# Feed-forward and output projection two chunks behind the attention; the right-hand matrix quantised beside chunks 0 to 2

## The chip, the cores and the metric

One Trainium2 chip runs the program on eight cores at once. A core has five engines with a program each: PE (TensorE, matmuls and transposes), DVE (VectorE), ACT (ScalarE), POOL (GpSimd) and SP (SyncE, which here only issues DMAs). They meet through semaphores. The metric is the device time of the slowest core in microseconds.

## The reference

```
x  [16, 2048, 1024]
xn = layernorm(x)
q, k, v = xn @ Wq.T, xn @ Wk.T, xn @ Wv.T      # 16 heads of 64
a  = softmax(q k / 8, position i sees i-127 .. i) v
s  = a @ Wo.T
ql = clip(round(xn / lhs_scale)), lhs_scale = max|xn| over the row / 127
qr = clip(round(rhs / rhs_scale)), rhs_scale = max|rhs| over the column / 127
g  = silu((ql @ qr) * lhs_scale * rhs_scale)
out = x + s * g
```

Each core has two of the 16 sequences, that is 4096 rows, and all five weight matrices of 1024 x 1024.

## The kernel before

The rows are worked on in 32 chunks of 128 (`NC`); two chunks make a span. A chunk c needs: the layer norm (`bn` the statistics, `rstd` the root on POOL, `xn` the normalised tile in bf16), its transpose (`TX`), Q and K for a span (`Q`, `K`, four groups each), V (`V`, two halves), the attention in four steps b of four heads (`S` scores, `exp` on ACT, `msk` on DVE, `A` product with V, `norm` on DVE), the quantised left-hand tile (`cen` on ACT, `amax` on DVE, `qp` on ACT, `ql` on DVE) and its transpose (`TL`), the feed-forward product (`F`, two halves: `zev` on DVE, `th` on ACT, `gate` on DVE), the output projection (`O`, two halves: `t1` on DVE, `add` on POOL) and the store. `t_xn`, `t_ql` and `t_ao` are DMA transposes that SP issues from chunk 4 or 6 on; before that PE transposes.

All orders are written out by hand. `pe_order` gives PE's list: a start in which Q, K, V follow the arrival of the weights, then for each chunk four slots. A slot is scores (c, b), the attention product of the step before, and the groups that `slot_gaps(c)` names for it. Before, F is of the same chunk and O of the one before; in a middle chunk the four slots hold two of Q or K; two of Q or K and V half 0; V half 1 and F half 0; F half 1 and both O.

Groups go to PSUM banks in turn: four banks `pj` for the ordinary ones, and in the start four more (`pav`, `psc`, list `early`). `before[g]` is the group four places back in the same list, and `pe_ready` lets g start only when that one has been emptied. Who empties is in `evacuator`: DVE for F and O, ACT for V, Q and K of later spans. `emit_vector`, `emit_scalar` and `emit_gpsimd` walk through the same slots; what a slot's groups leave for DVE comes after `msk`, `bn` or `xn` and `amax` of that slot, and the last one of a chunk is held until the next slot begins.

The right-hand matrix (`rhst`) comes in eight blocks. `rabs` and `rscale` (DVE) find the scales, `rq` (ACT) and `rcast` (POOL) quantise, `TR` transposes on PE, `RS` with `rdiag` spreads the scales. The staging tiles `stage` borrow `gg`, `zz`, `tt` and `xr`; the rounded blocks borrow `aot` and `ao`. `load_w` issues weight blocks from POOL; they are converted to bf16 on the way.

## Time and profile before

| what | value |
|---|---|
| times of three runs | 710.5, 711.29, 712.15 us; median 711.29 |
| the profiled execution | 712.11 us, span of the slowest core 710.5 us |
| spans of the eight cores | 703.9 to 710.5 us |
| granted TensorE clock, by core | 0.985 to 0.989 |
| PE busy | 665.4 us, 94% |
| DVE, ACT, POOL busy | 475.9, 346.7, 172.6 us |
| DMA moved | 86.40 MB |

The span is the time from the first to the last instruction of a core. The granted clock is 1.00 at 2.4 GHz, 0.5 at 1.2 GHz; a mean between is a mixture. A timeline row gives the start in us from the span's beginning, the length, the engine, the line and operation, output and inputs with their tile names, and how many equal instructions were merged; what stands in brackets is how long the engine was idle before it, and what ended that.

### The profile page before, as it was taken

The numbers are of one execution on the slowest core, as the hardware profiler recorded it, in microseconds if no ns is written. First come the engines' busy times: TensorE is split into PE (matmuls) and PEld (weight loads), VectorE is DVE, ScalarE is ACT, GpSimd is POOL, SyncE is SP. The second block draws the span as 40 slices with busy tenths as digits, with TensorE's granted clock in tenths as the row PEclk, the third lists the DMA queues.
The fourth block names the chain that finished last, engine by engine and source line by source line (L and its number), as shares of the span: only waits on it lengthen the run. The fifth ranks groups of instructions, "written<-read, shape, count | busy, mean of one in ns | idle before, by whom it ended". The sixth has DMA issues, their size and how long they took to land.

```text
span 710.5 us, 17009 instructions; the slowest of 8 cores (703.9 to 710.5 us)
## 1 busy us (share of the span) xinstructions
PE 665.4 (94%) x5724; PEld 413.0 (58%) x5724; DVE 475.9 (67%) x958; ACT 346.7 (49%) x473; POOL 172.6 (24%) x281
## 2 busy tenths in 40 slices
PE   1897769989999999999999999999999999999995
PEld 0682436555666666565666666565666666556642
DVE  4644577766776677766766667766766677664485
ACT  1342665544554445554554445554554445453442
POOL 4323311322222222121222222121222222120122
PEclk9998979999999999999999999999999999999999
DMA  9999913735655454656757445545555445543234
GB/s 191 149 200 188 182 18 76 149 119 134 134 129 127 119 88 97 131 120 134 134 120 127 115 102 94 130 120 134 135 122 125 115 92 104 131 89 76 76 90 149
DMA packets 109859, 86.40 MB, mean 122 GB/s; under 512 B 92112, under 2 KB 92240, under 8 KB 109776
## 3 DMA queue, kind: packets, MB, share of 16 engines
q1 hardware_dynamic: 104880, 76.83, 47.4%
q0 software_dynamic: 4608, 8.39, 8.4%
q8 instruction: 49, 0.80, 0.5%
q14 instruction: 34, 0.28, 0.1%
q10 hardware_dynamic: 288, 0.10, 0.1%
HBM read 54.62 MB, written 16.78 MB: 100 GB/s over the span
## 4 chain that ended last, share of the span: by engine, by line
PE 87%; DVE 5%; DMA 4%; issue 2%; POOL 1%; ACT 1%; DVEq 0%; SPq 0%; ACTq 0%; POOLq 0%
PE pj L675 44%; PE pj L666 29%; PE psc L759 5%; PE pav L783 4%; PE pav L785 2%; DMA xs<-x 2%; DMA wv<-wvt 2%; DVE ee L356 1%; PE pav L666 1%; PE psc L666 1%; DVE sm L326 1%; DVE gg L385 0%; DVE sm L291 0%; DVE sm L403 0%; POOL aot L831 0%
## 5 line engine op out<-in xcount | busy, mean ns | idle before, releaser
L573 ACT ACTIVATE ee<-psc 128x1024 bf16<-128x1024 f32 (+1 forms) x128 | 128.4, 1003 | 157.8 <-PE psc L759 152.9
L825 POOL TENSOR_TENSOR xr<-tt,xr 128x512 f32<-128x512 f32 x63 | 80.4, 1277 | 370.0 <-DVE tt L391 344.6
L675 PE MATMUL pj<-wv,xnt 128*128 128x512 bf16 x480 | 118.7, 391 | 5.1 <-DMA wv<-wvt 3.8
L675 PE MATMUL pj<-qrhs,qlt 128*128 128x512 bf16 x512 | 122.0, 382 | 0.0
L675 PE MATMUL pj<-wo,aot 128*128 128x512 bf16 x512 | 116.4, 379 | 1.2 <-ACT aot L313 1.2
L666 PE MATMUL pj<-xnt,wq 128*128 128x256 bf16 x960 | 112.3, 276 | 1.9 <-DVE xnt L311 1.8
L666 PE MATMUL pj<-xnt,wk 128*128 128x256 bf16 x960 | 109.7, 273 | 0.0
L356 DVE TENSOR_TENSOR ee<-ee,mask_s 128x1024 bf16<-128x1024 bf16 (+1 forms) x128 | 104.1, 813 | 7.6 <-ACT ee L573 2.1
L666 PEld LDWEIGHTS pj<-xnt,wq 128*128 128x128 bf16 x960 | 93.1, 99 | 13.5 <-issue 2.1
L666 PEld LDWEIGHTS pj<-xnt,wk 128*128 128x128 bf16 x960 | 92.0, 98 | 10.3
L675 PEld LDWEIGHTS pj<-wo,aot 128*128 128x128 bf16 x512 | 49.5, 98 | 60.0 <-issue 1.7
L391 DVE TENSOR_TENSOR tt<-pj,gg 128x512 f32<-128x512 f32 x64 | 44.0, 690 | 54.4 <-PE pj L675 53.4
L675 PEld LDWEIGHTS pj<-qrhs,qlt 128*128 128x128 bf16 x512 | 48.3, 99 | 54.3 <-issue 2.8
L675 PEld LDWEIGHTS pj<-wv,xnt 128*128 128x128 bf16 x480 | 45.9, 100 | 53.1 <-issue 12.0
L539 ACT ACTIVATE xs<-xs,sm 128x1024 f32<-128x1024 f32 x32 | 36.6, 1148 | 75.5 <-DVE xnr L321 75.5
L367 DVE TENSOR_TENSOR ao<-pav,sm 128x256 bf16<-128x256 f32 x128 | 54.4, 425 | 13.3
L326 DVE TENSOR_REDUCE sm<-xs 128x1 f32<-128x1024 f32 x32 | 39.0, 1218 | 34.9 <-ACT xs L539 34.9
L759 PEld LDWEIGHTS psc<-qt,kt 64*128 64x128 bf16 x992 | 28.1, 94 | 49.6 <-issue 49.4
L378 DVE SCALAR_TENSOR_TENSOR zz<-pj,sm,rsb 128x512 f32<-128x512 f32 x64 | 47.8, 747 | 10.7 <-PE pj L675 7.8
L759 PE MATMUL psc<-qt,kt 64*128 64x128 bf16 x992 | 50.1, 219 | 2.5 <-ACT ee L573 2.5
L783 PE MATMUL pav<-vv,ee 128*128 128x65 bf16 x480 | 46.5, 196 | 6.0 <-DVE ee L356 3.4
L556 ACT CAST kt<-pj 128x512 bf16<-128x512 f32 x60 | 33.6, 582 | 32.2 <-PE pj L666 32.2
(122 smaller groups left out, 661.5 us busy)
## 6 DMA issues: line engine op xcount, KB each, us to landing
xs<-x SPq DMA_DIRECT2D x32, 512.0 KB, 6.7
xr<-x SPq DMA_DIRECT2D x32, 512.0 KB, 7.2
y<-xr SPq DMA_DIRECT2D x31, 512.0 KB, 8.2
wq<-wqt POOLq DMA_DIRECT2D x8, 256.0 KB, 10.4
wk<-wkt POOLq DMA_DIRECT2D x8, 256.0 KB, 11.1
wv<-wvt POOLq DMA_DIRECT2D x8, 256.0 KB, 8.3
wo<-wot POOLq DMA_DIRECT2D x8, 256.0 KB, 10.1
xr<-rhst SPq DMA_DIRECT2D x3, 512.0 KB, 5.8
```

The costliest lines, as they stand in the source:

```text
L326: op(lambda: v.reduce_max(col(c, AMAX), xs[c % XS][:], AX.X, apply_absolute_value=True), "v")
L356: op(lambda: v.tensor_tensor(a, a, m, ALU.mult), "v", ("mask", c, b))
L367: op(lambda: v.tensor_tensor(view(ao[c % 2], b * 256, (64, 4), (1, 64)), view(p, 0, (66, 4), (1, 64)), bass.AP(sm, C_RS + 4 * (b % 2), [[1 ...
L378: op(lambda: v.scalar_tensor_tensor(zz[h], banks[bank["F", c, h]], col(c, LSH), rsb[:, h * 512:(h + 1) * 512], ALU.mult, ALU.mult), "v", ( ...
L391: op(lambda: v.tensor_tensor(tt[h], banks[bank["O", c, h]], gg[c % 2][:, h * 512:(h + 1) * 512], ALU.mult), "v", ("ev", "O", c, h))
L539: op(lambda: a.activation(xs[c % XS][:], xs[c % XS][:], AF.Identity, scale=-1.0, bias=col(c, MEAN)), "a", ("cen", c))
L573: op(lambda: a.activation(o, i, AF.Exp, scale=0.125), "a", ("exp", c, b))
L666: yield [(lambda kc=kc, m=m: t.matmul(p[:, m * 256:(m + 1) * 256], w[:, kc * 1024 + (2 * j + m) * 128:kc * 1024 + (2 * j + m + 1) * 128], ...
L675: yield [lambda kc=kc: t.matmul(p[:], src[:, off + kc * step:off + kc * step + 128], w[:, kc * 1024 + j * 512:kc * 1024 + (j + 1) * 512], ...
L759: todo.append(lambda m=m, kk=kk, ko=ko, rows=rows, q0=q0: t.matmul(psc[:, q0:q0 + 128], kk[rows, m * 256 + ko:m * 256 + ko + 128], qt[s % ...
L783: todo.append(lambda out=out, e0=e0, vp=vp: t.matmul(out, e[:, e0:e0 + 128], vp, start=True, stop=False))
L825: op(lambda: p.tensor_tensor(r, tt[h], r, ALU.add), "p", ("add", c, h))
```

## The change

- F and O are worked on in the slots of the chunk two later (`LAG`), through the whole program. Chunks 30 and 31 hold F and O of 28 and 29; F and O of 30 and 31 follow the last attention product (`last_groups`), and the last chunk's attention output is transposed by DMA like the others (`TA` goes).
- A middle chunk's four slots hold: F half 0 and one of Q or K; F half 1 and two of Q or K; the fourth of Q or K, V half 0 and O half 0; V half 1 and O half 1.
- x of chunks 0 to 3 is loaded in halves of 64 partitions, one half issued by SP and one by ACT. POOL issues the first Wq blocks once the first half of x(0) has landed, and Wk and Wv without a wait for `rhst`.
- The V groups of chunks 0 to 3, which came before the attention, now lie in the slots of chunk 0. `rhst` is loaded after Wv; its blocks are quantised in chunks 1 and 2, now with `rq_p` and `rcast` both on POOL, into other borrowed tiles. Wo is issued last, in two fours between those operations.
- Transposes of xn and ql for chunks 4 and 5 are emptied by ACT; those of ql go up to chunk 5 (`NTL`). Rings for small values and for ql transposes get longer (`NSM`, `QLR`). Statistics of chunk c + 4 begin in chunk 3.

```diff
@@ -16,12 +16,12 @@
...
-XS, XR, QLR, VR, NSM = 4, 3, 6, 6, 6
+XS, XR, QLR, VR, NSM, LAG = 4, 3, 7, 6, 8, 2
...
-C_MAGIC, C_NHALF, C_RST, C_RAM, C_RSC, C_RS = 144, 146, 148, 156, 164, 176
-NPRE, NTL = 6, 4
+C_MAGIC, C_NHALF, C_RST, C_RAM, C_RSC, C_RS, SMT = 192, 194, 196, 204, 212, 224, 240
...
@@ -47,22 +47,29 @@
...
     x = [("KQ"[c % 2 == 0], s + 1, g) for g in range(4)]
-    v, f, o = halves("V", c + 2), halves("F", c), halves("O", c - 1)
+    v, f, o = halves("V", c + 2), halves("F", c - LAG), halves("O", c - LAG)
     if c == 0:
-        return [halves("TX", 4, 5), halves("V", 4)[:1], halves("V", 4)[1:], []]
+        v2, v3 = halves("V", 2), halves("V", 3)
+        return [v2 + halves("TX", 4), v3 + halves("TX", 5), halves("TL", 4, 5), []]
     if c == 1:
-        v, f1 = halves("V", 5), [("F", i, 1) for i in range(2)]
-        return [halves("TR", 4, 5), v[:1] + halves("TR", 6, 7), v[1:] + [("RS", 0, 1)] + f1[:1], f1[1:]]
+        v4, v5 = halves("V", 4), halves("V", 5)
+        return [v4[:1], v4[1:] + halves("TR", 0, 1), v5[:1], v5[1:] + halves("TR", 2, 3)]
     if c == 2:
-        o0 = halves("O", 0)
-        return [x[:2], x[2:] + o0[:1], o0[1:] + o[:1], o[1:] + f]
+        return [x[:1] + [("RS", 0, 0)] + halves("TR", 4), x[1:2] + halves("TR", 5), x[2:3] + halves("TR", 6),
+                x[3:] + halves("TR", 7) + [("RS", 0, 1)]]
     if c == 3:
-        return [x[:2], x[2:], f[:1], f[1:] + o]
-    if c == NC - 2:
+        f0, o0 = halves("F", 0), halves("O", 0)
+        return [f0[:1] + x[:1], f0[1:] + x[1:2], f[:1] + x[2:3], x[3:] + f[1:] + o0]
+    if c == 4:
+        return [halves("O", 1) + x[:1], f[:1] + x[1:3], f[1:] + x[3:] + v[:1], v[1:] + o]
+    if c >= NC - 2:
         return [f[:1], f[1:], o[:1], o[1:]]
-    if c == NC - 1:
-        return [f[:1], f[1:], o[:1] + [("TA", c, 0)], o[1:] + [("TA", c, 1)]]
-    return [x[:2], x[2:] + v[:1], v[1:] + f[:1], f[1:] + o]
+    return [f[:1] + x[:1], f[1:] + x[1:3], x[3:] + v[:1] + o[:1], v[1:] + o[1:]]
+def last_groups():
+    return [g for k in "FO" for g in halves(k, *range(NC - LAG, NC))]
...
@@ -71,33 +78,27 @@
...
-    v0, v1 = halves("V", 0, 1), halves("V", 2, 3)
+    v0 = halves("V", 0, 1)
     each = lambda gs, steps: [("G", [g], steps) for g in gs]
-    out = one(halves("TX", 0, 1)) + [("G", q0, range(4))] + one(halves("TX", 2)) + [("G", q0, range(4, 5))]
-    out += one(halves("TX", 3)) + [("G", q1, range(5)), ("G", q0, range(5, 6)), ("G", q1, range(5, 6))]
-    out += each(q0 + q1, range(6, 8))
+    out = one(halves("TX", 0, 1)) + [("G", q0, range(6))] + one(halves("TX", 2, 3))
+    out += each(q0, range(6, 8)) + each(q1, range(8)) + one(halves("TL", 0, 1))
     out += [("G", k0, range(4)), ("G", k1, range(4))] + each(k0 + k1, range(4, 8))
-    out += one(halves("TL", 0, 1))
-    out += [("G", v0, range(4)), ("G", v1, range(4))] + each(v0 + v1, range(4, 8))
-    out += one(halves("TL", 2, 3) + halves("TR", 0, 1, 2, 3) + [("RS", 0, 0), ("F", 0, 0), ("F", 1, 0)])
-    for c in range(NC):
+    out += one(halves("TL", 2, 3))
+    first = slot_gaps(0)
+    for b, ks in enumerate((range(3), range(3, 6), range(6, 8))):
+        out += [("S", 0, b), ("G", v0, ks)]
+    out += [("A", 0, 0)] + one(first[0]) + [("S", 0, 3), ("A", 0, 1)] + one(first[1]) + [("A", 0, 2)] + one(first[2])
+    for c in range(1, NC):
         for b, gap in enumerate(slot_gaps(c)):
-            out.append(("S", c, b))
-            if b:
-                out.append(("A", c, b - 1))
-            elif c:
-                out.append(("A", c - 1, 3))
-            out += one(gap)
-    last = halves("O", NC - 1)
-    out += [("A", NC - 1, 3)] + one([("TA", NC - 1, 2)])
-    out += [("G", [g], range(6)) for g in last] + one([("TA", NC - 1, 3)])
-    out += [("G", [g], range(6, 8)) for g in last]
-    return out
+            out += [("S", c, b), ("A", c, b - 1) if b else ("A", c - 1, 3)] + one(gap)
+    return out + [("A", NC - 1, 3)] + one(last_groups())
...
+    if k in ("TX", "TL") and i >= 4:
+        return "a"
...
@@ -117,8 +118,8 @@
...
-    early = halves("TX", 2, 3) + [("Q", 1, g) for g in range(4)] + [("K", 1, g) for g in range(4)]
-    early += halves("V", 2, 3) + halves("TL", 2, 3) + halves("TR", 0, 1, 2, 3) + [("RS", 0, 0)]
+    wide = halves("TX", 2, 3) + halves("TL", 0, 1, 2, 3) + [(k, 1, g) for k in "QK" for g in range(4)]
+    early = [g for g in groups if g in wide]
@@ -195,23 +196,28 @@
...
+        def load_half(eng, c, h):
+            r = slice(h * 64, h * 64 + 64)
+            op(lambda: eng.dma_start(xs[c][r, :], x_h[c * 128 + h * 64:c * 128 + h * 64 + 64, :]),
+               f"{('lx', 'lh')[h]}{c}", c, 16)
...
@@ -248,37 +254,48 @@
         def load_rh(sync, i):
             if i == 7:
-                need(sync, "p", ("rcast", 3))
-            op(lambda: sync.dma_start(stage[i][:], rhst_h[i * 128:(i + 1) * 128, :]), f"rh{i % 7}", i, 16)
+                need(sync, "p", ("rcast", 0))
+            op(lambda: sync.dma_start(stage[i], rhst_h[i * 128:(i + 1) * 128, :]), f"rh{i}", 0, 16)
...
             for c in range(4):
-                load_x(sync, c)
-            landed(sync, "wk4", 0)
+                load_half(sync, c, 0)
+            landed(sync, "wk5", 0)
+            load_x(sync, 4)
+            load_x(sync, 5)
+            landed(sync, "wv4", 0)
             for i in range(4):
                 load_rh(sync, i)
-            landed(sync, "wv2", 0)
-            load_x(sync, 4)
-            load_x(sync, 5)
-            landed(sync, "wv6", 0)
+            load_x(sync, 6)
             for i in range(4, 8):
                 load_rh(sync, i)
-            load_x(sync, 6)
-            for c in range(NC):
...
-                    t_ao(sync, c - 1)
-                if 2 <= c < NC - 5:
+            load_x(sync, 7)
...
@@ -442,60 +458,61 @@
...
             evac_v(v, ("TL", 1, 0))
-            rabs(v, 3)
-            rscale(v, 2)
-            rdiag(v, 0)
             bn(v, 4)
             bn(v, 5)
+            evac_v(v, ("K", 1, 0))
+            evac_v(v, ("K", 1, 1))
+            xn(v, 4)
+            evac_v(v, ("K", 1, 2))
+            evac_v(v, ("K", 1, 3))
             evac_v(v, ("TL", 2, 0))
             evac_v(v, ("TL", 3, 0))
-            for i in range(4):
-                evac_v(v, ("TR", i, 0))
-            xn(v, 4)
             xn(v, 5)
-            rabs(v, 4)
-            zev(v, 0, 0)
-            rabs(v, 5)
-            rscale(v, 4)
-            gate(v, 0, 0)
-            zev(v, 1, 0)
-            rabs(v, 6)
-            gate(v, 1, 0)
-            extra = {(0, 1): [(rabs, 7), (rscale, 6)], (0, 2): [(rdiag, 1)], (0, 3): [(amax, 4)], (1, 1): [(ql, 4)],
-                     (1, 2): [(amax, 5)], (2, 0): [(ql, 5)]}
+            amax(v, 4)
+            msk(v, 0, 0)
+            amax(v, 5)
+            msk(v, 0, 1)
+            ql(v, 4)
+            msk(v, 0, 2)
+            ql(v, 5)
+            norm(v, 0, 0)
+            rabs(v, 0)
+            rabs(v, 1)
+            norm(v, 0, 1)
+            msk(v, 0, 3)
+            rscale(v, 0)
+            norm(v, 0, 2)
+            rabs(v, 2)
+            extra = {(1, 0): [(rabs, 3), (rscale, 2), (rdiag, 0)], (1, 1): [(rabs, 4)], (1, 2): [(rabs, 5), (rscale, 4)],
+                     (1, 3): [(rabs, 6)], (2, 0): [(rabs, 7), (rscale, 6)], (2, 1): [(rdiag, 1), (bn, 6)],
+                     (2, 3): [(xn, 6)], (3, 0): [(amax, 6)], (3, 1): [(ql, 6)]}
             held, gates = None, []
...
@@ -601,36 +619,37 @@
...
+            evac_a(a, ("TL", 0, 1))
+            evac_a(a, ("TL", 1, 1))
             for g in range(4):
                 ev_qk(a, "K", 0, g)
-            rq(a, 0)
-            rq(a, 1)
-            evac_a(a, ("TL", 0, 1))
-            evac_a(a, ("TL", 1, 1))
-            rq(a, 2)
-            rq(a, 3)
-            for g in halves("V", 0, 1, 2, 3):
+            cen(a, 4)
+            evac_a(a, ("TL", 2, 1))
+            evac_a(a, ("TL", 3, 1))
+            ex(a, 0, 0)
+            cen(a, 5)
+            qp(a, 4)
+            ex(a, 0, 1)
+            qp(a, 5)
+            ex(a, 0, 2)
+            first = slot_gaps(0)
+            for g in halves("V", 0, 1) + first[0]:
                 evac_a(a, g)
-            for g in halves("TL", 2, 3) + halves("TR", 0, 1, 2, 3) + [("RS", 0, 0)]:
+            ex(a, 0, 3)
+            for g in first[1] + first[2]:
                 evac_a(a, g)
-            cen(a, 4)
-            cen(a, 5)
-            rq(a, 4)
-            th(a, 0, 0)
-            rq(a, 5)
-            th(a, 1, 0)
-            extra = {(0, 1): [(rq, 6)], (0, 2): [(rq, 7)], (1, 0): [(qp, 4)], (1, 3): [(qp, 5)]}
+            extra = {(2, 3): [(cen, 6)], (3, 0): [(qp, 6)]}
...
@@ -824,11 +835,15 @@
...
+        def rq_p(p, i):
+            need(p, "v", ("rsc", i - i % 2))
+            st = stage[i]
+            op(lambda: p.tensor_scalar(st, st, sm[:, C_RSC + i:C_RSC + i + 1], MAGIC, ALU.mult, ALU.add),
+               "p", ("rq", i))
         def rcast(p, i):
-            need(p, "a", ("rq", i))
-            if i >= 4:
-                need(p, "t", ("TR", i - (4 if i < 6 else 2), 1))
-            op(lambda: p.tensor_scalar(rst_bf[i][:], stage[i][:], -MAGIC, 1.0, ALU.add, ALU.mult),
+            own(p, "p")
+            op(lambda: p.tensor_scalar(rst_bf[i], stage[i], -MAGIC, 1.0, ALU.add, ALU.mult),
                "p", ("rcast", i))
@@ -838,34 +853,32 @@
...
+            landed(p, "lx0", 0)
             load_w(p, 0, range(2))
-            need(p, "v", ("bn", 0))
+            rstd(p, 0)
             load_w(p, 0, range(2, 4))
-            rstd(p, 0)
+            rstd(p, 1)
             load_w(p, 0, range(4, 8))
-            rstd(p, 2)
+            rstd(p, 2, 2)
             load_w(p, 1, range(8))
-            landed(p, "rh1", 0)
-            load_w(p, 2, range(4))
-            rcast(p, 0)
-            rcast(p, 1)
-            load_w(p, 2, range(4, 8))
-            rcast(p, 2)
-            rcast(p, 3)
-            rstd(p, 4)
-            landed(p, "rh6", 0)
-            load_w(p, 3, range(8))
-            for i in range(4, 8):
+            load_w(p, 2, range(8))
+            rstd(p, 4, 2)
+            for i in range(8):
+                rq_p(p, i)
                 rcast(p, i)
+                if i == 5:
+                    load_w(p, 3, range(4))
+            load_w(p, 3, range(4, 8))
+            rstd(p, 6)
...
```

How PE's list changes in a middle chunk, where DVE's evacuations are waited for. Before, the second slot of chunk 4: `pav` is the end of an attention product, then two Q groups (`wq`) and V half 0 (`wv`).

```order
L785 MATMUL pav0<-vv4,ee0 128x65
L666 MATMUL pj1<-xnt1,wq 128x256 [waits s_v]
L666 MATMUL pj1<-xnt1,wq 128x256 x15
L666 MATMUL pj2<-xnt1,wq 128x256 [waits s_v]
L666 MATMUL pj2<-xnt1,wq 128x256 x15
L675 MATMUL pj3<-wv,xnt1 128x512 [waits s_a,s_txn0]
L675 MATMUL pj3<-wv,xnt1 128x512 x7
L759 MATMUL psc<-qt0,kt1 128x128 [waits s_a]
```

After, the third slot of chunk 5, from the end of its attention product on, with K group 3 (`wk`), V half 0 and O half 0 (`wo`):

```order
L797 MATMUL pav1<-vv5,ee1 128x65
L685 MATMUL pj1<-xnt1,wk 128x256 [waits s_a]
L685 MATMUL pj1<-xnt1,wk 128x256 x15
L694 MATMUL pj2<-wv,xnt1 128x512 [waits s_v,s_txn1]
L694 MATMUL pj2<-wv,xnt1 128x512 x7
L694 MATMUL pj3<-wo,aot1 128x512 [waits s_a,s_tao1]
L694 MATMUL pj3<-wo,aot1 128x512 x7
L771 MATMUL psc<-qt0,kt0 128x128 [waits s_a]
```

Before, V half 0 waits for ACT's semaphore (`s_a`), which has emptied `pj3`; now it goes into `pj2` and waits for DVE's (`s_v`), which empties `pj2` of F half 1.

DVE's list in the same place, from the statistics' join of chunk c + 4 on. Before (`gg` is the gate, `ao` the norm, `ee` the mask, `xnr` the normalised tile, the reduction and the small ones `amax`):

```order
L293 BN_AGGR sm<-sm 128x2 [waits s_v]
L385 SCALAR_TENSOR_TENSOR gg0<-gg0,zz 128x512 [waits s_a]
L365 RECIPROCAL sm<-pav0 128x4 [waits s_t,s_tao1]
L367 TENSOR_TENSOR ao1<-pav0,sm 128x256 [waits s_v]
L356 TENSOR_TENSOR ee1<-ee1,mask_s 128x1024 [waits s_a]
L321 TENSOR_SCALAR xnr1<-xs1,sm 128x1024 [waits s_p,s_txn1]
L326 TENSOR_REDUCE sm<-xs1 128x1 [waits s_a]
L329 TENSOR_SCALAR sm<-sm 128x1 [waits s_p,s_v]
L331 RECIPROCAL sm<-sm 128x1 [waits s_v]
L332 TENSOR_SCALAR sm<-sm 128x1
L334 TENSOR_SCALAR sm<-sm 128x1 [waits s_v]
L365 RECIPROCAL sm<-pav1 128x4 [waits s_t]
```

After, in chunk 5 (`zz<-pj0` and `zz<-pj2` are the evacuations of F half 0 and half 1):

```order
L393 SCALAR_TENSOR_TENSOR zz<-pj0,sm,rsb 128x512 [waits s_t,s_v]
L381 RECIPROCAL sm<-pav0 128x4 [waits s_t,s_tao1]
L383 TENSOR_TENSOR ao1<-pav0,sm 128x256 [waits s_v]
L372 TENSOR_TENSOR ee1<-ee1,mask_s 128x1024 [waits s_a]
L400 SCALAR_TENSOR_TENSOR gg1<-gg1,zz 128x512 [waits s_a]
L337 TENSOR_SCALAR xnr1<-xs1,sm 128x1024 [waits s_p,s_txn1]
L342 TENSOR_REDUCE sm<-xs1 128x1 [waits s_a]
L345 TENSOR_SCALAR sm<-sm 128x1 [waits s_p,s_v]
L347 RECIPROCAL sm<-sm 128x1 [waits s_v]
L348 TENSOR_SCALAR sm<-sm 128x1
L350 TENSOR_SCALAR sm<-sm 128x1 [waits s_v]
L393 SCALAR_TENSOR_TENSOR zz<-pj2,sm,rsb 128x512 [waits s_t,s_v]
```

The gate that followed the join is a zev now, the gate stands in front of xn, and the second zev comes straight after amax, where a norm was.

DVE's list in the start, where the statistics of chunks 4 and 5 stand. Before, they are behind everything that K needs, and the transposes of ql and of the right-hand matrix follow:

```order
L291 BN_STATS sm<-xs 128x6 x2
L293 BN_AGGR sm<-sm 128x2
L291 BN_STATS sm<-xs 128x6 x2
L293 BN_AGGR sm<-sm 128x2
L311 COPY qlt<-pav 128x512
L311 COPY qlt<-psc 128x512
L311 COPY qrhs<-pav 128x4x128
L311 COPY qrhs<-psc 128x4x128
L311 COPY qrhs<-pav 128x4x128
L311 COPY qrhs<-psc 128x4x128
L321 TENSOR_SCALAR xnr<-xs,sm 128x1024 x2
```

After, the evacuations of K of span 1 (`kt`) come behind them, two before and two behind xn of chunk 4:

```order
L359 TENSOR_SCALAR qlr<-xs 128x1024 x2
L310 BN_STATS sm<-xs 128x6 x2
L312 BN_AGGR sm<-sm 128x2
L310 BN_STATS sm<-xs 128x6 x2
L312 BN_AGGR sm<-sm 128x2
L445 CAST kt<-pav 128x512 x2
L337 TENSOR_SCALAR xnr<-xs,sm 128x1024
L445 CAST kt<-psc 128x512 x2
L327 COPY qlt<-pav 128x512
L327 COPY qlt<-psc 128x512
L337 TENSOR_SCALAR xnr<-xs,sm 128x1024
```

POOL's list in the start. Before, casts (`aot`, `ao`) of blocks that ACT has rounded lie between the Wv issues:

```order
L837 DMA wk<-wkt 128x1024 x8
L837 DMA wv<-wvt 128x1024 x4
L831 TENSOR_SCALAR aot0<-gg0 128x1024
L831 TENSOR_SCALAR aot1<-gg1 128x1024
L837 DMA wv<-wvt 128x1024 x4
L831 TENSOR_SCALAR ao0<-zz 128x1024
L831 TENSOR_SCALAR ao1<-tt 128x1024
L808 TENSOR_SCALAR sm<-sm 128x2
L810 TENSOR_TENSOR sm<-sm 128x2
L812 TENSOR_TENSOR sm<-sm 128x2
```

After, all Wv issues come at once, then the root for chunks 4 and 5, and then pairs of rounding (`gg0<-gg0,sm`) and cast:

```order
L852 DMA wk<-wkt 128x1024 x8
L852 DMA wv<-wvt 128x1024 x8
L819 TENSOR_SCALAR sm<-sm 128x2
L821 TENSOR_TENSOR sm<-sm 128x2
L823 TENSOR_TENSOR sm<-sm 128x2
L825 TENSOR_TENSOR sm<-sm 128x2
L827 TENSOR_SCALAR sm<-sm 128x2
L829 TENSOR_TENSOR sm<-sm 128x2
L841 TENSOR_SCALAR gg0<-gg0,sm 128x1024
L846 TENSOR_SCALAR aot1<-gg0 128x1024
L841 TENSOR_SCALAR gg1<-gg1,sm 128x1024
```

POOL no longer waits for ACT between weight blocks; it rounds the blocks itself.

## Rows read from the trace of the kernel before

**Rows 1.** The page: busy time by engine; two costly groups (busy, mean ns, idle before).
```profile
PE 665.4 (94%) x5724; PEld 413.0 (58%) x5724; DVE 475.9 (67%) x958; ACT 346.7 (49%) x473; POOL 172.6 (24%) x281
...
L356 DVE TENSOR_TENSOR ee<-ee,mask_s 128x1024 bf16<-128x1024 bf16 (+1 forms) x128 | 104.1, 813 | 7.6 <-ACT ee L573 2.1
...
L326 DVE TENSOR_REDUCE sm<-xs 128x1 f32<-128x1024 f32 x32 | 39.0, 1218 | 34.9 <-ACT xs L539 34.9
```

**Rows 2.** The span in stretches: length, busy time of engines, PE clock, DMA share, GB/s.
```profile
0.00:54.34 54.34, 34.15 (x305) 29.56 (x305) 29.39 (x69) 19.42 (x25) 19.68 (x42) 1.00 0.97 179
54.34:156.75 102.41, 86.33 (x652) 47.33 (x653) 66.14 (x139) 51.48 (x71) 23.75 (x38) 0.90 0.62 125
156.75:677.58 520.83, 520.83 (x4546) 324.39 (x4546) 356.42 (x708) 263.42 (x360) 120.86 (x197) 1.00 0.52 114
677.58:705.05 27.47, 23.99 (x225) 11.76 (x224) 21.44 (x41) 12.39 (x17) 7.08 (x6) 1.00 0.47 135
705.05:710.50 5.45, 0.12 (x1) 0.00 (x0) 2.53 (x3) 0.00 (x0) 1.26 (x1) 0.89 0.26 96
```

**Rows 3.** Timeline of PE: start, us, instructions; first transposes, and sixteen in a row.
```profile
14.92 1.86 PE L660 MATMUL pj<-ident_s,xnr 128*128 128x128 bf16 x16 [14.92 <-DVE xnr L321]
...
100.08 1.05 PE L660 MATMUL pj<-ident_s,aot 128*128 128x128 bf16 x16
```

**Rows 4.** DMA issues inside 53.12:53.20 and 24.50:25.15: size, median us to landing.
```profile
xs<-x SPq DMA_DIRECT2D x1, 512.0 KB, 11.2
...
wk<-wkt POOLq DMA_DIRECT2D x3, 256.0 KB, 13.4
```

**Rows 5.** Timeline of POOL: first and last step of a root for two chunks.
```profile
66.21 0.19 POOL L808 TENSOR_SCALAR sm<-sm 128x2 f32<-128x2 f32 x1 [5.20 <-DVE sm L293]
...
68.44 0.20 POOL L818 TENSOR_TENSOR sm<-sm 128x2 f32<-128x2 f32 x1
```

**Rows 6.** Timeline of PE in a middle chunk: scores, and one V group.
```profile
436.78 0.40 PE L759 MATMUL psc<-qt,kt 64*128 64x128 bf16 x8
...
440.95 0.40 PE L759 MATMUL psc<-qt,kt 64*128 64x128 bf16 x8
...
446.85 0.40 PE L759 MATMUL psc<-qt,kt 64*128 64x128 bf16 x8
...
447.43 1.89 PE L675 MATMUL pj<-wv,xnt 128*128 128x512 bf16 x8
...
450.98 0.40 PE L759 MATMUL psc<-qt,kt 64*128 64x128 bf16 x8
...
456.84 0.40 PE L759 MATMUL psc<-qt,kt 64*128 64x128 bf16 x8
```

**Rows 7.** Timeline of DVE in that chunk, from the statistics to the next norm.
```profile
439.67 1.27 DVE L291 BATCH_NORM_STATS2 sm<-xs 128x6 f32<-128x512 f32 x2
441.05 0.21 DVE L293 BATCH_NORM_AGGREGATE sm<-sm 128x2 f32<-128x12 f32 x1
...
444.66 0.81 DVE L321 TENSOR_SCALAR xnr<-xs,sm 128x1024 bf16<-128x1024 f32 x1 [1.25 <-POOL sm L818]
446.82 1.22 DVE L326 TENSOR_REDUCE sm<-xs 128x1 f32<-128x1024 f32 x1 [1.34 <-ACT xs L539]
...
448.91 0.17 DVE L365 RECIPROCAL sm<-pav 128x4 f32<-128x4 f32 x1
```

**Rows 8.** Timeline of POOL in that chunk: first step of the root.
```profile
441.42 0.47 POOL L808 TENSOR_SCALAR sm<-sm 128x1 f32<-128x1 f32 x1 [2.22 <-DVE sm L293]
```

**Rows 9.** Timeline of DVE after the last matmul.
```profile
704.98 1.29 DVE L391 TENSOR_TENSOR tt<-pj,gg 128x512 f32<-128x512 f32 x2 [4.21 <-PE pj L675]
706.37 1.32 DVE L399 TENSOR_TENSOR xr<-tt,xr 128x512 f32<-128x512 f32 x1
```

**Rows 10.** Timelines of POOL and of DVE: a cast and a zev at one time.
```profile
87.93 1.04 POOL L831 TENSOR_SCALAR aot<-xr 128x1024 bf16<-128x1024 f32 x1 [0.50 <-ACT xr L550]
...
88.08 0.75 DVE L378 SCALAR_TENSOR_TENSOR zz<-pj,sm,rsb 128x512 f32<-128x512 f32 x1
```

165 lines of the change are left out of this document (83 added, 82 removed).

## The prediction

> **What bounds the kernel now.** I read the page first. The TensorE (PE) is busy for 665.4 of 710.5 us [rows 1], so only its waits, its slow clock and the ends can be won. The stretches of the span come next [rows 2]. From 156.75 to 677.58 us PE is busy for all of 520.83 us at clock 1.00: 26 chunks of 20.06 us [rows 6], with no wait. Before that lie 54.34 us up to the first V group (34.15 busy), then 102.41 us up to the scores of chunk 4, with 86.33 busy at clock 0.90; at the end 27.47 us with 23.99 busy, and 5.45 us after the last matmul. Third, the timeline: PE starts at 14.92 us, held by the first normalised tile [rows 3]. So the kernel is PE-bound with poor ends, and a change of order pays at the ends and can only lose in the middle.
>
> Unit costs, from one chunk's four slots [rows 6]. The slot with two Q groups takes 4.17 us, the one with a V group besides 5.90, so a V, F or O group is 1.73. The slot with V and F takes 4.13, which leaves 0.67 for scores and attention product, 2.7 a chunk, and 1.75 for a Q or K group. The first group of a slot starts 0.58 after its scores. Four transposes are 0.25 (16 in 1.05 [rows 3]; 0.47 is the upper end, from the row that has waits in it). A column sum I take at 0.9, half of a group to two groups being its bounds; two of them decide nothing.
>
> **The change part by part.**
>
> *Up to the scores of chunk 0.* In halves on two queues the first x tiles come earlier, and so does PE's first transpose, perhaps at 10 instead of 14.9. But Q of span 0 still needs all eight Wq blocks, whose bytes and those of x are the same (DMA share 0.97 over this stretch [rows 2]); I leave the last of them near 25.5. From there Q, K and the transposes need 0.9 + 7 + 1 + 14 + 1 = 24, which gives 49.5 for the end of that work. DVE then ends last. In its program the statistics of chunks 4 and 5 now stand ahead of the evacuations of K span 1, and x(5) is issued only when the sixth Wk block has landed. The last three Wk blocks land 13.4 us after issues at about 24.6, so at 38, and the sixth at 36 to 37; the second x tile issued among weight blocks took 11.2 us [rows 4]. With a start some 0.8 earlier that is 46.5. Then 1.6 for the statistics, 2.4 for POOL's root (66.21 to 68.64), 0.8 for xn(4), 1.3 for two K evacuations and 1.0 for the transposes and their evacuation (the last two estimated from the sizes of their neighbours) [rows 5, 7]: first scores at 53.4. Bounds: 50.5 (x early, PE sets it) and 56 (x(5) a weight block or two later). Before, V(0) started at 54.34 with the same matmuls behind it except the transposes.
>
> *Chunks 0 to 3.* PE's work from 53.4 to the scores of chunk 4: chunk 0 has 8 V groups, 8 transpose groups and half pairs, 17.1; chunk 1 has 4 V, 8 transpose groups, 2.7, so 11.6; chunk 2 has 4 Q, 8 transpose groups, 2 sums, 2.7, so 13.5; chunk 3 has 4 K, 6 F or O, 2.7, so 20.1. Sum 62.3. Added waits, worked out by following each engine's program with the durations of the rows: 0.9 in chunk 0 (V evacuations on ACT behind the exponentials). 2.5 in chunk 1, where DVE has four masks with norms at 1.3, four absolute maxima at 1.2 [rows 1], and two scales, the diagonal and four evacuations, which I put at 4: 14 us for 11.6 of PE. 0.9 in chunk 2. 2.0 at F(0,0): its bank is Q(2,3)'s, whose evacuation on ACT stands behind cen(6), xn(6) and POOL's root of chunk 6, which POOL reaches only after the two casts of blocks 6 and 7 and four Wo issues. 3.0 in chunk 3, where DVE makes the maxima of chunks 6 and 7 and two zev, and mask(3,2) comes late. And the clock: 54.34:156.75 costs about 10 us at 0.90. After a stand of 3 to 4 us at 49.5, and one of 3 in chunk 3, I take 2.5 and 1.7, bounds 0 and 10. That gives 13.5; scores of chunk 4 at 53.4 + 62.3 + 13.5 = 129.2, bounds 123 and 136. What is behind them is more than before: F and O are two chunks late.
>
> *The root, casts and quantisation on POOL.* The eight quantisations leave ACT and cost POOL what a cast costs or more; the mean stays hidden, since rcast(0) to (7) fall in pairs behind each scale and PE asks for a pair once in some 8 us. In ACT nothing is won, because ACT does not bound this part.
>
> *The middle.* Work of chunk 4 is 2.7 + 7 + 8 groups = 23.5; chunks 5 to 29 are 25 x 20.06, less 1.35 for chunk 16 = 500.2; chunks 30 and 31 have 9.6 each; then 8 groups of 1.73. Sum 556.7. **Here stands the new wait.** A projection bank is used again four groups later. From chunk 5 on V(c+2,0) takes the bank of F(c-2,1), with Q or K, Q or K, Q or K between. DVE empties F(c-2,1), but its program has xn(c+4) and amax(c+4) ahead of that. Take the chunk at 436.78. Its amax chain ends where the next DVE work can start, at 448.91, that is 12.13 us after the chunk's first scores [rows 6, 7]. Everything on that chain has the same order before and after: t1, norm, mask, statistics to 441.26, POOL's root, xn at 444.66, cen, reduction at 446.82 [rows 7, 8]. The only difference is a zev in place of a gate. The zev takes 0.75 [rows 10] and a PE start follows an evacuation by about 0.2 (estimated): V may start at 13.08. PE is there after a slot with F and one Q (4.15), one with F and two (5.90), 0.58 and a Q group: 12.38. So PE waits 0.7 us in each of chunks 5 to 27 (28 and 29 have no amax left; in chunks 3 and 4 the banks fall otherwise): 23 x 0.7 = 16.1. Bounds: 0.6 (POOL's root not stretched by the gate, 0.1 earlier) and 1.05. Nothing later in the chunk hangs on it: mask(c,2) is due 3 us later, t1 waits for PE. The stand is short, and the last 27.47 us kept the clock at 1.00 with 3.5 us of waits in them [rows 2]; I price no clock loss.
>
> *The end.* Before, chunks 30 and 31 with O(31) and its transposes by PE took 27.47 for 23.2 of work. The same slots keep some 1.65 of waits (masks behind POOL's adds); the two stands on aot copies go, since eight dense groups cover the DMA transpose. After the last matmul only one t1 is left and the add finds POOL done: 5.45 becomes 4.2 [rows 2, 9]; bounds 3.6 and 5.5.
>
> **Sum.** 129.2 + 556.7 + 16.1 + 1.65 + 4.2 = 707.9 of span, against 710.5. The profiled execution took 712.11 (span + 1.6), 0.8 over the median of 711.29, so the forecast is 708.7. In short: about 18.7 us are won at the ends and 16 given back in the middle.
>
> The Trainium skill weighs in on the wait: SBUF — State Buffer, "Who interferes with whom", says that a DVE operation with two SBUF inputs, or in a two-port mode, and a GpSimd operation exclude each other for their whole length. Here the first instruction of the root took 0.47 beside a gate, and a cast beside a zev (one operand from PSUM) kept its 1.04 [rows 8, 10]; by that rule, the trace agrees, the zev frees the root and the wait is 0.6, the sum 705.6. The same skill, DMA: Bandwidth & Descriptors, "Issuing engines are not separate DMA queues", says that all issuing engines share the same DMA engines and that more of them only save issue time; no run here has x on two queues. By it the halves bring no bytes earlier; the sum already has none.
>
> **Rivals.**
> *No wait for the bank.* If DVE reaches F(c-2,1) in time, which needs the chain to end 0.7 us sooner, the middle stays at 20.06 a chunk and the span is 691.8, time 692.6. For it: before, the same chain just fits. Against it: each of its links is in the rows.
> *The wait is larger (slower).* If the zev stretches POOL's first step and then the masks and the gate each stretch one of the next, the root ends 0.35 later (the first step takes 0.47 instead of 0.19 [rows 5, 8]). Then V waits 1.05 in 23 chunks, 24.2 in all, and the time is 716.8. It decides from 0.81 us a chunk on, where 23 waits eat the 18.7 of the ends. The first part could put it there too: each us lost in it moves that point down by 0.04. For it: the root has been stretched in every chunk shown. Against: the trace shows no stretch by a zev [rows 10].
> *The start wins more.* If x(4), x(5) land early, PE sets the first scores (50.5), and if the clock stays up (4.2 less): 707.9 - 2.9 - 4.2, so about 701.6 as a time.
>
> **How the numbers follow.** Forecast 0.56, with 702 to 715 as its own range, which lies on both sides of the old time (0.27 faster, 0.12 the same, 0.17 slower); no wait 0.14; larger wait 0.20; better start 0.10. 0.2% (1.4 us) is what a measurement of this kernel can tell. Faster: 0.27 + 0.14 + 0.10 = 0.51; same 0.12; slower 0.17 + 0.20 = 0.37. The range is 694 to 719: the lower end is near the no-wait case with somewhat more lost, the upper one the larger wait with 2 us more in the first part.
>
> **What would show it.** Waits of PE: a row "V matmul waits for the zev of DVE", 23 times at about 0.7. In PE's timeline a chunk of 20.75 instead of 20.06, and 20.06 in chunks 28 and 29. First scores of chunk 0 near 53, of chunk 4 near 129, an ACT or DVE wait of about 2 at F(0,0). No aot wait at the end, and 4.2 us after the last matmul. I am wrong if chunks take 20.06, or if the scores of chunk 4 are outside 123 to 136.

## The result and the profile after

The changed kernel takes 731.04 us (728.78 to 731.32, 4 runs) against 710.89 for the kernel before: a ratio of 1.0274, interval 1.0249 to 1.03. It is slower, and 731 lies outside the range of 694 to 719. Some executions of this program fall into a slower state of the chip; all times and ratios here are of the others. The profiled execution took 731.3 us, its span is 729.7; rows below are of its slowest core, core 5, unless another is named.

The span in stretches, against [rows 2] (length, busy time of PE, PEld, DVE, ACT, POOL, PE clock, DMA share, GB/s). The cuts are the first scores of chunk 0, of chunks 4, 5 and 30, and the end of PE.

```profile
0.00:60.71 60.71, 37.53 (x321) 30.81 (x321) 31.84 (x74) 19.88 (x26) 21.25 (x52) 0.96 1.00 184
60.71:142.66 81.95, 70.20 (x590) 41.12 (x590) 55.61 (x120) 43.04 (x64) 26.52 (x37) 0.93 0.52 117
142.66:168.76 26.10, 23.67 (x193) 13.95 (x192) 16.54 (x31) 10.96 (x15) 6.78 (x11) 1.00 0.45 122
168.76:689.39 520.63, 504.44 (x4369) 310.14 (x4368) 359.98 (x680) 254.28 (x346) 114.51 (x189) 1.00 0.44 110
689.39:725.90 36.51, 33.70 (x265) 15.85 (x264) 28.54 (x51) 12.79 (x16) 9.68 (x8) 1.00 0.41 114
725.90:729.70 3.80, 0.00 (x0) 0.00 (x0) 1.34 (x2) 0.00 (x0) 0.40 (x1) 0.76 0.58 224
```

PE's largest waits in the whole program (engine, line, what it waited for, us in total, times, longest):

```profile
PE pj L694 <- DVE sm L381: 16.2, 23, 0.9
PE pj L679 <- DVE xnr L337: 15.6, 2, 12.7
PE pav L795 <- DVE ee L372: 7.1, 8, 2.5
PE pj L685 <- DVE sm L381: 3.8, 2, 2.4
PE psc L679 <- DVE kt L445: 2.7, 1, 2.7
```

The first row is the forecast wait: V (L694) in 23 chunks, 16.2 us. The releaser's name needs care. L381 is the reciprocal that stands behind the zev in DVE's program; a view that infers names from semaphores can be one instruction off. Chunk 18 shows it. PE's timeline there, from the third scores on (K or Q group, V, O, fourth scores):

```profile
449.81 0.40 PE L771 MATMUL psc<-qt,kt 64*128 64x128 bf16 x8
...
450.39 1.91 PE L685 MATMUL pj<-xnt,wq 128*128 128x256 bf16 x16
453.18 1.89 PE L694 MATMUL pj<-wv,xnt 128*128 128x512 bf16 x8 [0.87 <-DVE sm L381]
454.90 1.89 PE L694 MATMUL pj<-wo,aot 128*128 128x512 bf16 x8
456.72 0.40 PE L771 MATMUL psc<-qt,kt 64*128 64x128 bf16 x8
```

DVE's timeline in the same place, the last two steps of the maximum and the zev that frees the bank:

```profile
451.73 0.15 DVE L348 TENSOR_SCALAR sm<-sm 128x1 f32<-128x1 f32 x1 [0.22 <-issue]
451.99 0.21 DVE L350 TENSOR_SCALAR sm<-sm 128x1 f32<-128x1 f32 x1
452.17 0.75 DVE L393 SCALAR_TENSOR_TENSOR zz<-pj,sm,rsb 128x512 f32<-128x512 f32 x1
```

The zev ends at 452.92, V starts 0.26 later. From chunk 5 on nearly all chunks with an odd number take 20.77 us and those with an even number 21.10 (20.07 before), in all eight cores alike.

The longest pieces of the early part of the chain of work that ended last (start, us, what):

```profile
1.50 5.97 DMA xs<-x
23.65 3.66 POOL wk L852 x5
27.31 13.31 DMA wk<-wkt
41.23 11.23 DMA xs<-x
```

The fourth line is x(5), issued only after the sixth Wk block (third line) had landed, at 40.62. It lands at 52.46. PE was nearly done with K by then, and stood (L679: transposes of ql, L771: first scores):

```profile
53.24 0.93 PE L685 MATMUL psc<-xnt,wk 128*128 128x256 bf16 x7
54.98 0.88 PE L679 MATMUL pav<-ident_s,qlr 128*128 128x128 bf16 x8 [0.81 <-DVE kt L445]
58.60 1.08 PE L679 MATMUL psc<-ident_s,qlr 128*128 128x128 bf16 x8 [2.74 <-DVE kt L445]
60.71 0.40 PE L771 MATMUL psc<-qt,kt 64*128 64x128 bf16 x4 [1.03 <-ACT qlt L329]
```

All eight cores agree: the first scores start 8.05 to 8.25 us after x(5) has landed, and 4.9 to 7.5 us after the end of K. The slowest core is late here, 60.7 us against a median of 58.2 over the cores.

So there are two separate losses: a wait in every middle chunk, and a start in which little was won. To the scores of chunk 4 the new kernel needs 142.66 us instead of 156.75, but it has left eight F and O groups (13.8 us) for later. Net that is 0.3 us (1.2 us between the medians of the cores, 139.6 and 154.7).

### The profile page after: what moved, and what is told of

It is laid out like the page before. It is cut to its first block, busy times and chain, and to the rows that moved or that the text cites. A ratio compares the mean times of both kernels' runs of the same rounds, so it can differ in the third digit from the quotient of the medians.

```text
span 729.7 us, 17049 instructions; the slowest of 8 cores (725.6 to 729.7 us)
## 1 busy us (share of the span) xinstructions
PE 669.5 (92%) x5732; PEld 411.9 (56%) x5732; DVE 493.9 (68%) x956; ACT 340.9 (47%) x467; POOL 179.1 (25%) x295
## 4 chain that ended last, share of the span: by engine, by line
PE 41%; DVE 23%; issue 16%; POOL 9%; ACT 5%; DMA 4%; DVEq 1%; POOLq 0%; ACTq 0%; SPq 0%
PE pj L694 32%; DVE sm L310 5%; DVE sm L342 4%; ACT xs L561 4%; PE pj L685 4%; DVE xnr L337 3%; DMA xs<-x 2%; POOL sm L821 2%; POOL sm L825 2%; PE psc L771 2%; DMA wk<-wkt 2%; DVE tt L407 2%; POOL sm L827 2%; DVE ao L383 1%; DVE sm L381 1%
## 5 line engine op out<-in xcount | busy, mean ns | idle before, releaser
L836 POOL TENSOR_TENSOR xr<-tt,xr 128x512 f32<-128x512 f32 x63 | 79.7, 1266 | 402.3 <-DVE sm L381 353.2
L694 PE MATMUL pj<-wv,xnt 128*128 128x512 bf16 x512 | 122.6, 384 | 17.5 <-DVE sm L381 16.2
L372 DVE TENSOR_TENSOR ee<-ee,mask_s 128x1024 bf16<-128x1024 bf16 (+1 forms) x128 | 123.9, 968 | 15.2 <-ACT ee L589 9.3
L694 PE MATMUL pj<-qrhs,qlt 128*128 128x512 bf16 x512 | 120.5, 379 | 0.9 <-ACT qrhs L329 0.8
L694 PE MATMUL pj<-wo,aot 128*128 128x512 bf16 x512 | 120.0, 379 | 0.0
L685 PE MATMUL pj<-xnt,wq 128*128 128x256 bf16 x960 | 115.1, 277 | 4.6 <-DVE sm L381 3.8
L685 PE MATMUL pj<-xnt,wk 128*128 128x256 bf16 x960 | 115.5, 277 | 0.3 <-DVE qlt L327 0.3
L685 PEld LDWEIGHTS pj<-xnt,wk 128*128 128x128 bf16 x960 | 94.6, 100 | 18.7 <-issue 0.4
L694 PEld LDWEIGHTS pj<-wv,xnt 128*128 128x128 bf16 x512 | 46.7, 98 | 71.7 <-issue 26.5
L694 PEld LDWEIGHTS pj<-wo,aot 128*128 128x128 bf16 x512 | 49.7, 98 | 59.3
L694 PEld LDWEIGHTS pj<-qrhs,qlt 128*128 128x128 bf16 x512 | 46.2, 98 | 47.3 <-issue 1.2
L595 ACT ACTIVATE gg<-zz 128x512 f32<-128x512 f32 x64 | 40.3, 630 | 44.3 <-DVE sm L381 35.7
L578 ACT CAST vv<-pj 128x512 bf16<-128x512 f32 x64 | 37.4, 589 | 39.1 <-PE pj L694 34.9
L572 ACT CAST qt<-pj 128x512 bf16<-128x512 f32 x60 | 33.2, 578 | 47.2 <-PE pj L685 47.2
## 6 DMA issues: line engine op xcount, KB each, us to landing
wk<-wkt POOLq DMA_DIRECT2D x8, 256.0 KB, 11.4
```

Source lines behind the costliest of these rows:

```text
L372: op(lambda: v.tensor_tensor(a, a, m, ALU.mult), "v", ("mask", c, b))
L572: op(lambda: a.copy(dst[:, g * 512:(g + 1) * 512], banks[bank[k, s, g]]), "a", ("ev", k, s, g))
L595: op(lambda: a.activation(gg[c % 2][:, h * 512:(h + 1) * 512], zz[h][:], AF.Tanh), "a", ("tanh", c, h))
L685: yield [(lambda kc=kc, m=m: t.matmul(p[:, m * 256:(m + 1) * 256], w[:, kc * 1024 + (2 * j + m) * 128:kc * 1024 + (2 * j + m + 1) * 128], ...
L694: yield [lambda kc=kc: t.matmul(p[:], src[:, off + kc * step:off + kc * step + 128], w[:, kc * 1024 + j * 512:kc * 1024 + (j + 1) * 512], ...
L836: op(lambda: p.tensor_tensor(r, tt[h], r, ALU.add), "p", ("add", c, h))
```

## The experiments

Two theories were to be told apart for each loss. Middle: the wait is only DVE's order, or DVE has no room. Start: one late transfer and the order of a few instructions, or DMA and DVE as such.

**F emptied before the maximum** (`e1_zev_first`):

```diff
+                    first = [g for g in gap if g[0] == "F"] if ln and b == 1 and c >= 4 else []
                     if ln and b == 1:
                         xn(v, c + 4)
+                        for g in first:
+                            evac_v(v, g)
                         amax(v, c + 4)
...
                     for g in todo:
-                        evac_v(v, g)
+                        if g not in first:
+                            evac_v(v, g)
```

> From chunk 4 on DVE empties the F group of the second slot before it takes the absolute maximum of chunk c + 4 (after xn, where it waited 1.35 us for cen anyway). Theory (the bank wait is nothing but DVE's order): the 16.2 us of waits of V in 23 chunks and the 2.4 us in chunk 4 go, chunks 5 to 29 fall from 20.77 and 21.1 to 20.06 us, the time from 731.0 to about 709. Rival (DVE has no room in these chunks, the wait only moves to the masks or to V's second half): chunks stay above 20.6, time above 722. Second rival (the alternation 20.77 / 21.10 has a cause of its own): odd chunks 20.06, even ones 20.4, time about 713.

Measured: 706.9 us, ratio to the kernel before 0.9945 (0.9928 to 0.9962). Against the changed kernel's 731.04 that is 24 us less. Chunks 5 to 29 take 20.07 each, odd and even (16 and 17 are shorter, 19.27 and 19.95, as before the change), and chunk 4 23.52 instead of 26.10. DVE's timeline of chunk 18 there: xn, zev, maximum and the first small step behind it:

```profile
432.75 0.81 DVE L337 TENSOR_SCALAR xnr<-xs,sm 128x1024 bf16<-128x1024 f32 x1 [0.56 <-POOL sm L833]
433.48 0.74 DVE L393 SCALAR_TENSOR_TENSOR zz<-pj,sm,rsb 128x512 f32<-128x512 f32 x1
434.91 1.22 DVE L342 TENSOR_REDUCE sm<-xs 128x1 f32<-128x1024 f32 x1 [0.69 <-ACT xs L565]
436.59 0.21 DVE L345 TENSOR_SCALAR sm<-sm 128x1 f32<-128x1 f32 x1 [0.46 <-DVE sm L342]
```

The maximum had waited 1.35 us for ACT's cen all along; the zev now lies in that gap and delays nothing. The stall of the even chunks is still there: 0.46 us instead of 0.11 before L345, where the bank no longer hangs on it. Both rivals fall: the wait did not move, and the alternation went with it. DVE was never short of time in the middle; it had the wrong thing first.

**x(4) and x(5) issued at the second Wk block** (`e2_x45_early`), one line of SP's program:

```diff
...
-            landed(sync, "wk5", 0)
+            landed(sync, "wk1", 0)
...
```

> SP issues x(4) and x(5) once the second Wk block has landed (31.4 us) instead of the sixth (40.6 us). Theory (the first scores wait for x(5), which lands at 52.5 us, while PE has ended K at 54.2): x(5) lands near 42 us, first scores at 56.2 to 57 instead of 60.7, everything later the same, time about 727. Rival (the two tiles take their 1 MB from Wk and K becomes late): last Wk block at 46 instead of 43.1, PE waits in K, first scores at 59 to 61, time 730 to 731.

Measured: 726.17 us, ratio 1.0212 (1.0186 to 1.0239), so 4.9 us less than the changed kernel. Over the eight cores the median landing of x(5) moves from 50.2 to 43.1 and that of the first scores from 58.2 to 55.6. The last Wk block lands 3 us later (44.0, was 40.9), as the rival said, but no wait for it shows on PE. In all eight cores the first scores now start 2.53 us after the end of K, and x(5) has landed 11.4 to 14.8 us before them. The slowest core, after K:

```profile
52.18 0.61 PE L679 MATMUL pav<-ident_s,qlr 128*128 128x128 bf16 x8
52.97 0.88 PE L679 MATMUL psc<-ident_s,qlr 128*128 128x128 bf16 x8 [0.18 <-issue]
54.88 0.29 PE L771 MATMUL psc<-qt,kt 64*128 64x128 bf16 x4 [1.03 <-DVE xnr L337]
```

**Wv held back** (`e3_wv_held`): a wait for the fourth Wk block before the Wv issues.

> POOL issues the Wv blocks once the fourth Wk block has landed, not right behind Wk. Theory (Wv's packets share the DMA engines with Wk's, whose blocks landed 3.8 and 2.8 us apart instead of 1.3): the sixth Wk block lands at about 38 instead of 40.6, x(5) near 49.5 instead of 52.5, first scores at 58 to 59 instead of 60.7, time 728 to 729. Rival (the blocks of one queue land in order, Wv takes nothing from them): sixth Wk block at 40.6, first scores at 60.7; Wv lands later but is not waited for, time 731; if Wv is then waited for in chunk 0, 732 to 734.

Measured: 729.99 us, ratio 1.0274 (1.024 to 1.0308), no difference. The sixth Wk block landed at 39.0 in the slowest core and x(5) at 51.3, within the spread of the cores. Wv takes nothing measurable from Wk; the rival holds.

**Rounding on ACT** (`e4_rq_act`): `rq_p` on POOL becomes an activation on ACT in chunks 1 and 2.

> ACT rounds the blocks of the right-hand matrix, as in the kernel before, in chunks 1 and 2; POOL only casts. Theory (chunks 1 and 2 are bound by DVE, whose masks take 1.2 to 1.4 us beside POOL's rounding and casts against 0.69 alone): with half of POOL's work gone, three or four masks get 0.5 us shorter, scores of chunk 1 to scores of chunk 3 take 31 us instead of 33.2, time about 729. Rival (ACT's exponentials get later by the 1.15 us of each rounding): 34 to 35 us, time 732 to 733.

Measured: 731.32 us, ratio 1.0292 (1.0255 to 1.0328), no difference. In the slowest core chunks 1 and 2 took 32.3 instead of 33.2, but that core is the exception: in the other seven of the changed kernel they take 31.0 to 31.1. Here all eight take 32.0 to 32.4, so they got longer by some 1.2: the rival's direction, though not its 34 us. The wait at F(0,0) is 2.1 to 2.3 us here; in the changed kernel it is 0.8 in the slowest core and 2.8 to 3.0 in the others.

**The two that helped, together, and two edits of order on top** (`f1_both`, `f2_root_before_wo`, `f3_max7_later`), the last two being:

```diff
# f2, POOL
...
-            load_w(p, 3, range(4, 8))
             rstd(p, 6)
+            load_w(p, 3, range(4, 8))
...
# f3, DVE in chunk 3 (and qp(7) on ACT one slot later)
-                        amax(v, c + 4)
+                        if c > 3:
+                            amax(v, c + 4)
                     if ln and b == 2:
-                        ql(v, c + 4)
+                        if c > 3:
+                            ql(v, c + 4)
+                        else:
+                            amax(v, 7)
+                    if c == 3 and b == 3:
+                        ql(v, 7)
...
```

> Both edits that helped: F emptied before the absolute maximum from chunk 4 on, and x(4), x(5) issued at the second Wk block. Theory (the two losses, the bank wait and the late first scores, are independent): 707.3 less 4.9, so 702 to 703, first scores near 55, chunks of 20.06. Rival (the earlier start is given back in chunk 3, which took 30.4 us instead of 27.1 in the run with x early, as F(0,0) waits for ACT behind chunk 6's root): 704 to 706.

> As the last one, and POOL takes the root of chunk 6 before it issues the last four Wo blocks. Theory (PE waits 2.8 us at F(0,0) for ACT's evacuations, which stand behind cen(6), xn(6) and that root, and the four issues hold the root 2.2 us): the wait falls below 0.7, time 2 us under the last one. Rival (DVE is the bound of chunk 3, so that the wait moves to mask(3,2), 2.5 us now): less than 0.7 us gained.

> As the last one, and the absolute maximum, the scaling on ACT and the rounding of chunk 7 one slot later, so that mask (3,2) no longer stands behind them. Theory (the 2.5 us at that mask come from DVE's order in chunk 3 alone): they go, and often a stretch at half clock behind them (1.7 us): 2.5 to 4 us under the last one. Rival (DVE has too much to do in chunk 3 in any order): the wait appears at the next mask or in chunk 4, under 1 us gained.

Measured: `f1_both` 703.17 us, ratio 0.9883 (0.9858 to 0.9908). The gains of e1 and e2, taken as ratios, add up to the same 0.9883, so the two losses are independent. `f2_root_before_wo` 703.30, 0.9891 (0.9859 to 0.9922), no difference. Here too the cores are of two kinds. In six of them the wait at F(0,0) fell from 2.8 or more to 1.1 or 1.3 us, and chunks 1 to 3 sum to 58.5 to 58.7 (most had 60). The slowest core is of the other kind, with 33.2 us for chunks 1 and 2: it has a wait of 1.4 at the first Q group of chunk 2, one of 0.8 at a transpose and one of 0.8 at F(0,0), and its sum is 60.3, as core 5 of the changed kernel has it. So the edit does what was expected in most cores, and not in the one that sets the time. `f3_max7_later` 699.61, 0.9832 (0.9806 to 0.9858): chunk 3 takes 24.02 instead of 27.11, and the second of the two half-clock stretches (at about 125 to 131 us, in all eight cores of `f2_root_before_wo`) is gone.

**Wq at once** (`f4_wq_at_once`), the wait for x(0) before the first two Wq issues taken out of the last version:

> As the last one, and POOL issues the first two Wq blocks at once, not after the first half of x(0). Theory (the start is paced by the bytes of x(0) to x(3) and Wq, 6 MB through DMA engines busy for 97 to 100%, whatever their order): the last Wq block lands at about 26 as before the edit, PE's first transpose some 2 us later than 12.7, first scores within 0.7 us, time the same. Rival (the DMA engines stand idle for the first 6 us, share 0.65, and each us filled is won): last Wq block and first scores 1.5 to 3 us earlier, time as much less.

Measured: 701.32 us, ratio 0.9854 (0.983 to 0.9879). The intervals of the ratios overlap, but all four runs lie above the four of the version before it, by 1.7 us in the median; in any case nothing is won. PE's first transpose comes 1.3 us later (14.1, median over the cores, was 12.9), the last Wq block at 27.7 as before.

**Four more on that version (699.61)**:

> The version with chunk 7's maximum one slot later (699.6 us), and ACT rounds the blocks of the right-hand matrix. Theory (DVE bounds chunks 1 and 2, and its masks take 1.2 to 1.4 us beside POOL's work against 0.69 alone; in the first test the gain was lost at F(0,0), a wait that is now short): chunks 1 and 2 from 33.3 to 32 us or less, chunk 3 unchanged, time 1 to 1.5 us less. Rival (the roundings hold up ACT's exponentials and evacuations as much): no change, 699 to 701.

> The same version with x(0) to x(3) as whole tiles issued by SP alone, as in the kernel before. Theory (the DMA engines are the bound up to the first scores, not the queues that issue): PE's first transpose 0.5 to 2 us later than 12.9, the last Wq block and the first scores within 0.7 us, time 699 to 701. Rival (two queues bring the first tiles and all behind them earlier): first scores 2 us later, time 701.5 to 702.

> The same version with the eight Wo issues right behind the root of chunks 4 and 5, ahead of the quantisation on POOL. Theory (Wo's bytes find room in chunks 0 and 1, where the DMA share is 0.65 and 0.30, and the 4.4 us of issues between POOL's casts go): the last casts 2.2 us earlier, chunk 2 at most 1 us shorter, time 698.5 to 700. Rival (Wo's 4 MB stand in front of the right-hand matrix, whose blocks land 5 to 8 us later, so that DVE's maxima in chunk 0 and all casts come late): chunk 1 and 2 longer by 2 to 5 us, time 702 to 705.

> The same version with DVE's maxima over the right-hand blocks 3 and 4 in chunk 0, where DVE is busy for 11.6 of 21.2 us, and those of 5 to 7 and the scales one slot earlier. Theory (chunks 1 and 2, 33.3 us for 25.1 of PE's work, are bound by DVE's program): they fall to 29 to 31 us, time 2 to 4 us less, near 696. Rival (they are bound by something else, such as the exponentials on ACT or the PSUM bank of the transposes): under 1 us gained.

Measured: ACT rounding 699.86 (0.9824, 0.9802 to 0.9845); whole tiles 699.76 (0.9821, 0.9799 to 0.9844); Wo early 700.63 (0.9836, 0.9815 to 0.9856); maxima in chunk 0 698.80 (0.9809, 0.9787 to 0.9832). None differs from its base by more than its interval. With ACT rounding chunks 1 and 2 took 32.3 us in the median core, where the base has 31.2: longer again, not the 32 or less from 33.3 that was expected of the slowest core. With Wo early the seventh right-hand block landed at 85.7 in place of 71.2 us, and no chunk of the slowest core got longer, so Wo's place decides nothing either way. With the maxima in chunk 0, chunks 1 and 2 fell from 33.3 to 31.9 in the slowest core and chunk 3 took 0.5 of that back; in the median core they fell from 31.2 to 30.6. I had hoped for 29 to 31 from 33.3.

**Parts undone on the changed kernel itself, and all together**:

> The changed kernel with one part undone: x(0) to x(3) as whole tiles, issued by SP alone. Theory (the halves of 64 partitions land later, the second one at 7.5 us instead of 5.2 for a whole tile, and so put off the first transpose and Wq, which POOL issues behind x): PE's first transpose at 10.5 to 11 instead of 12.7, the last Wq block at 24.3 to 25 instead of 26.4, first scores at 57.5 to 59 instead of 60.7, time 1.5 to 3 us under 731.0. Rival (only the DMA engines' bytes count, the first tiles decide nothing): last Wq block 26 to 26.5, time 730.5 to 731.5.

> The changed kernel with chunk 6's root before the last Wo issues and chunk 7's maximum, scaling and rounding one slot later, nothing else. Theory (the wait of 2.5 us at mask (3,2) and a stretch at half clock behind it come from that order): chunk 3 from 27.1 to 23.5 to 24.5 us, time 2.5 to 3.5 us under 731.0. Rival (the gain needs the early start of the other version, or is given back at the bank wait of chunk 4): under 1 us.

> All that helped in one kernel: F emptied first, x(4) and x(5) early, root of chunk 6 before Wo, chunk 7's maximum later, the maxima of the right-hand matrix in chunk 0, x in whole tiles. Theory (the parts are independent): first scores near 54.5, scores of chunk 4 near 130, time 696 to 697.5. Rival (DVE's order in chunks 1 to 3 takes back what comes earlier): 698.5 to 700.

Measured: `h1_whole_on_after` 729.9, ratio 1.0248 (1.0226 to 1.0269), not clearly different. Over the eight cores PE's first transpose comes at 11.3 instead of 12.5, so the halves made it later, not earlier; but the last Wq block lands at 26.5 (was 26.2), the first scores at 58.1 (was 58.2). The rival holds: x on two queues decides nothing. `h2_chunk3_alone` 726.93, 1.0209 (1.0187 to 1.0231), 4.1 us less than the changed kernel. PE before the fourth K group and F(1,1) of chunk 3, first in the changed kernel, then here:

```profile
130.79 0.40 PE L771 MATMUL psc<-qt,kt 64*128 64x128 bf16 x8 [0.26 <-ACT ee L589]
...
133.73 0.19 PE L795 MATMUL pav<-vv,ee 128*128 128x65 bf16 x1 [2.54 <-DVE ee L372]
...
133.98 3.56 PE L685 MATMUL pj<-xnt,wk 128*128 128x256 bf16 x16
```

```profile
128.75 0.40 PE L777 MATMUL psc<-qt,kt 64*128 64x128 bf16 x8 [0.49 <-ACT ee L595]
129.81 0.19 PE L801 MATMUL pav<-vv,ee 128*128 128x65 bf16 x1 [0.66 <-DVE ee L372]
...
130.05 1.91 PE L691 MATMUL pj<-xnt,wk 128*128 128x256 bf16 x16
```

The wait of 2.54 has shrunk to 0.66, and the K group behind it no longer runs at half clock (1.91 us for sixteen matmuls instead of 3.56). In two of the eight cores, the slowest among them, a half-clock stretch stands in chunk 4 (at 154.5 to 158.3 us), where the bank wait is still in place; two cores of the changed kernel have that one too.

`h3_all` 697.34 us (697.18 to 698.14), ratio 0.9795 (0.9775 to 0.9815): 2% faster than the kernel before, 34 us faster than the change as it stood. Its stretches:

```profile
0.00:56.81 56.81, 36.84 (x320) 30.91 (x321) 31.87 (x74) 19.73 (x26) 21.39 (x52) 0.97 0.97 173
56.81:131.22 74.41, 65.97 (x588) 39.27 (x589) 55.33 (x120) 43.00 (x64) 26.92 (x37) 0.98 0.61 145
131.22:154.74 23.52, 23.52 (x193) 14.07 (x194) 16.16 (x31) 10.81 (x15) 6.79 (x11) 1.00 0.55 139
154.74:655.50 500.76, 500.76 (x4369) 311.80 (x4369) 355.73 (x680) 254.86 (x346) 114.37 (x189) 1.00 0.47 114
```

The 500.76 us of chunks 5 to 29 are PE without a gap; the forecast's work for them was 500.2.

## Why the prediction was wrong

The sum came out 21.8 us short (729.7 against 707.9), and the scores of chunk 4 at 142.7 us lie outside the 123 to 136 that the prediction named as its own limit. By its own steps:

| step | forecast | measured | off by |
|---|---|---|---|
| first scores of chunk 0 | 53.4 | 60.7 (median core 58.2) | +7.3 |
| chunks 0 to 3 | 75.8 | 81.95 | +6.2 |
| chunk 4 | 23.5 | 26.1 | +2.6 |
| chunks 5 to 29, work and bank wait | 516.3 | 520.6 | +4.3 |
| chunks 30, 31, last groups, end | 38.9 | 40.3 | +1.4 |

*The bank wait* was right in kind, place and nearly in size, and e1 shows it by removing it. The step that the zev follows was forecast to end 12.13 us after the chunk's scores, and there the zev starts; it started 12.08 after them in chunk 5 and 12.41 in chunk 6. Odd chunks lost 0.71 as forecast (0.7). Even ones lost 1.03, because DVE stood 0.3 us longer inside the small steps of the maximum (row `[0.22 <-issue]` above). In all it was 19.9 us (520.63 less the 500.76 of the best version). Working from one chunk's rows of before could not show that: there the same steps ran without it, and DVE's stall of every second chunk stood before a reciprocal early in the chunk (0.20 us), where nothing hung on it. The rival of a larger wait named another mechanism (POOL's root stretched). The root did not get longer: from its first step to xn's start it took 3.15 us in chunk 6 (194.16 to 197.31) against 3.24 before [rows 7, 8]. Its first step, beside the zev, took 0.19 instead of the 0.47 beside a gate, but two later steps, beside the mask and the gate, took 0.67 and 0.44. Still the size of that rival, 1.0 us a chunk in 23, is what half of the chunks had.

*Chunk 4*: "in chunks 3 and 4 the banks fall otherwise" was wrong. In chunk 4 the fourth Q group takes the bank of F(2,0), whose zev stands behind the maximum just as later; PE waited 2.4 us, and e1 removed it.

*The first scores*: this is the step that failed most, "x(5) is issued only when the sixth Wk block has landed ... the sixth at 36 to 37". The order was read rightly, the time was not. I took the landings of before and set them 0.8 us earlier. The sixth Wk block landed at 40.62 (38.2 in the median core) instead of 36.3 before, since POOL issued Wk later:

```profile
20.98 0.19 POOL L819 TENSOR_SCALAR sm<-sm 128x2 f32<-128x2 f32 x1 [2.78 <-DVE sm L312]
...
23.65 5.28 POOL L852 DMA_DIRECT2D wk<-wkt  x8 [0.23 <-issue]
```

Before, the same root started at 18.23 and the Wk issues at 20.91:

```profile
18.23 0.20 POOL L808 TENSOR_SCALAR sm<-sm 128x2 f32<-128x2 f32 x1 [2.62 <-DVE sm L293]
...
20.91 5.08 POOL L837 DMA_DIRECT2D wk<-wkt  x8 [0.23 <-issue]
```

The root of chunks 2 and 3 waits for DVE's statistics. In the changed kernel DVE takes both behind xn(1) and its transposes' evacuation, from 17.66 us on, although x(3) had landed at 13.9. No run moves these statistics, so what that order alone costs is not shown. x(5) then landed at 52.5 in place of 46.5, and the first scores followed 8.3 us behind it, against my 6.9 (whose parts add up to 7.1, so that the sum should have said 53.6). e2 confirms the mechanism: x(5) 7 us earlier, first scores 2.6 us earlier on the median core (5.8 between the slowest cores of the two runs), no more, since then the end of K is the bound, 53.0 in the median core of either kernel where I had 49.5. So the rival of a better start, 50.5, was out of reach too.

*Chunks 0 to 3*: the waits I listed (9.3) summed to 11.8 in the slowest core. 1.1 in chunk 0, 2.9 in chunk 1 and 4.8 in chunk 3 are near my figures (0.9, 2.5, 5.0); chunk 2 had 2.9 instead of 0.9. The 4.8 hides a miss: F(0,0) waited only 0.8 there, for which I had 2.0. In the seven other cores it waited 2.8 to 3.0; core 3 has

```profile
113.36 3.31 PE L694 MATMUL pj<-qrhs,qlt 128*128 128x512 bf16 x8 [2.78 <-ACT qrhs L329]
```

The slow clock took about 5.9 instead of 4.2 (granted clock 0.89, 1.00, 0.91 and 0.94 in chunks 0 to 3), and the rest, some 2 us, is work that I had put too low, half of it in chunk 0 (18.1 for my 17.1). The place in chunk 3 was right (mask(3,2) behind the maximum of chunk 7): h2 and f3 remove most of it for 4 us. Chunks 1 and 2 stay 5 to 8 us over PE's work (25.1) in every version; of four edits aimed at them (e4, g1, g3, g4) the best gained 0.6 in the median core. That DVE bounds them is therefore not shown, and what does stays open. Core 5's 33.2 us go with a half-clock stretch in chunk 2; in cores 1, 2, 3, 4 and 7 it lies in chunk 1, in 0 and 6 in neither.

*The ends as a whole*: the sentence "18.7 us are won at the ends" is what sank the forecast. With the bank wait gone (e1) the kernel is 4 us faster than before, not 18. The tail gave 3.0 us: 2.5 of waits (7.3 over its work, 9.7 before) and 0.5 of work. The start up to the scores of chunk 4 gave 1.4 in that run and 0.3 in the changed kernel's own (1.2 in the median core of both), against a forecast of 13.7. The gain on paper stood on landing times, on waits of 9.3 that were 11.8 and on a K that ended 3.5 us later than reckoned; up to the first scores the DMA engines are busy for 97 to 100%, before, after and in the best version.

The direction was wrong for an avoidable reason: I had found a cost of 16 us that was certain in the rows and set against it a gain of 19 us that was a sum of estimates in the part of the program with the most unknowns. The chance of slower, 0.37, was too low for that.

*Two rules on sharing*: the masks of this run took longer beside POOL. In chunk 1 a mask of 0.69 us took 1.41 beside a cast, and the mean mask of the run rose from 813 ns [rows 1] to 968. The casts are not the cause of that rise: it comes from POOL's adds of O (L836), which stood beside 55 of the 128 masks in place of 32, and such a mask takes 1.31 us in the mean. With the zev in place of the gate the root's first step was freed, but the bank wait did not fall to 0.6 as the prediction's second sum had it; it was 0.71 and 1.03, for later steps of the root were stretched and the root got only 0.09 shorter. The Trainium skill's SBUF — State Buffer, "Who interferes with whom", says that a DVE instruction with two SBUF inputs contends with a GpSimd instruction that reads SBUF, and one with at most one SBUF input outside the two-port modes does not. That fits the masks, the freed first step and the two stretched later ones. The costly group of masks in the page of this run, then one mask and the cast beside it:

```profile
L372 DVE TENSOR_TENSOR ee<-ee,mask_s 128x1024 bf16<-128x1024 bf16 (+1 forms) x128 | 123.9, 968 | 15.2 <-ACT ee L589 9.3
```

```profile
92.23 1.41 DVE L372 TENSOR_TENSOR ee<-ee,mask_s 128x1024 bf16<-128x1024 bf16 x1
```

```profile
92.06 1.04 POOL L846 TENSOR_SCALAR zz<-tt 128x1024 bf16<-128x1024 f32 x1 [0.16 <-POOL tt L841]
```

Of x on two queues h1 and g2 show that it brings nothing: with halves the last Wq block lands at 26.2 us, with whole tiles at 26.5; for f3 and g2 it is 27.7 with halves and 25.9 with whole tiles, at the same time of the kernel. The Trainium skill's DMA: Bandwidth & Descriptors, "Issuing engines are not separate DMA queues", says that starting transfers from several engines saves only the time of issuing them; the runs agree.

## What to carry to other kernels

A PSUM bank that goes round a ring is as late as the slowest thing in front of its evacuation; when groups are reordered, list for every reuse what stands before the evacuation in its engine's program, and put the evacuation into a gap where that engine waits anyway. Here one moved call was worth 24 of 731 us. Weigh a cost that repeats in every chunk and is read from rows more heavily than a gain at the ends that rests on landing times not yet seen; and where a load waits for another load, ask first whether it has to. Look at all cores before an edit is judged by the slowest one: here chunks 1 and 2 take 33.2 us in core 5 and 31.1 in the other seven, and two edits that seemed to shorten them made them longer.

## What the runs showed of the hardware

- A stall of DVE of 0.2 to 0.35 us came once in two chunks at a fixed place of its program, in all cores alike: before a reciprocal (0.20 us) in the kernel before, inside the small steps of the maximum (0.22 us) in the changed one, behind the reduction of the even chunks (0.46 us instead of 0.11) in e1. It costs only where PE hangs on what follows. What it is stays open.
- Tiles of x in halves of 64 partitions on two queues: first tile complete at 6.6 to 7.5 us over the eight cores; as a whole tile on one queue (h1) at 4.6 to 7.8, and PE's first transpose 1.3 us sooner in the median core. The whole start was no faster for it.
- A wait of 2.5 us on PE in chunk 3 had a stretch of half clock (3.4 us) beginning within 1.2 us of its end, before or behind, in seven of eight cores; in h2, with the wait cut to 0.66 in the slowest core, no core had that stretch in chunk 3. The waits of 0.5 to 0.9 us in chunks 5 to 27 never did that: the clock is 1.00 from 168.76 to 689.39, and in the same chunks of the seven other cores.
